# Rotary products read from PSUM by VectorE, sums by GpSimd, q/k/v parts stored by half sequences

## The chip, the cores and the metric

The kernel runs on one core of a Trainium2 chip, in one launch. The metric is the device time of that launch in microseconds (us), the median of three runs. Engines are named as the profile names them: PE is TensorE, PEld its weight loads, DVE VectorE, ACT ScalarE, POOL GpSimd, SP the SyncE queue that issues DMAs.

## The reference, cut to what matters

The kernel computes one attention layer and one mixture-of-experts layer on x of shape (8, 1024, 256), in float32. Only the front of the attention layer is touched by the change:

```python
x = x + attn(layernorm(x))                 # then x + ffn(layernorm(x)), 8 experts, top-k tokens
q, kv = x @ Wq, x @ Wkv                    # 16 heads of 16 columns; kv is both keys and values
q, kv = rotary(q), rotary(kv)              # per head: t * cos + rotate_half(t) * sin
# rotate_half(t) = concat(-t[8:16], t[0:8]) within a head
att = softmax(q @ kv.T * 16 ** -0.5); out = att @ kv; out @ Wout + bout
```

## The kernel before, in words

The program has five stages that follow each other on every engine: **project** (the one that changes), attend, finish, choose and experts. All orders are written out by hand, engine by engine, and semaphores join them.

`project` handles the 8 sequences as 64 tiles of 128 tokens, two sequences (16 tiles) to a pass, 4 passes. For a tile the steps are: statistics and normalisation on DVE (L231 to L244), two PE transposes into `p_ps_xT` (L373), a copy to SBUF by ACT (L338), four matmul passes (PE, L381) into a PSUM bank of `p_ps_q` that holds q and kv side by side (512 columns), a copy of that bank to `p_qkv` in SBUF (ACT, L345), the rotary, four PE transposes into `p_ps_rT` (L391), and the cutting of the result into a high and a low part: ACT copies the high part, rounded to float32r (L354), DVE subtracts it for the low part (L272). ACT also copies the values (L355). The rotary is shared out: DVE multiplies `p_qkv` by cos (L254), POOL multiplies the swapped halves by sin in two instructions (L307), and the sum is made by DVE for the first 128 columns (L264) and by POOL for the other 384 (L317).

The order on each engine is a software pipeline: in the period of tile j an engine does step A for tile j minus the lag of A, step B for tile j minus the lag of B, and so on (`Flow`, L73; the lags stand in L109). So each engine walks through its list once for every tile, and a wait in any step holds back the steps behind it on that engine.

The parts of a sequence lie in `p_parts`, which has room for two sequences. When all 8 tiles of a sequence are cut, SP stores them to the DRAM tensor `qkv_parts` with 8 DMAs of 512 KB (L178; 128 rows of 4 KB each; the DRAM side has 8 heads as its first dimension, 16 rows and 1024 elements) and then the values with one DMA of 1 MB (L182). ACT may write the first tile of a sequence only when the parts and values of the sequence two before have landed (L351, L352). SP is one queue in program order: it also loads x in blocks of four tiles (L167), and it issues `load_first` (L209), which loads the first three pairs of heads for the attend stage (L528, L534, and the rows of ones, L553). In the last pass `load_first` stands before the stores of that pass.

`attend` works on 64 pairs of heads. PE starts with the score maxima of pair 0 (L709, needs the loads of pair 0 and the end of the project stage on PE and DVE), DVE reduces them (L761), the maxima are turned into rows and put into `a_q` by a DMA that ACT issues for pair 0 (L543), and only then do the scores of pair 0 start (L672). For pair 1 the same DMA is issued by SP, which first waits for all stores of the project stage (`stored`, L213).

## Time and profile before

| | us |
|---|---|
| three runs, median (lowest to highest) | 2242.66 (2234.14 to 2255.21) |
| the profiled execution | 2249.14 |
| its span | 2247.3 |
| PE, DVE, ACT, POOL busy | 2015.3, 1947.7, 1503.4, 649.2 |
| last cut of the project stage (DVE, L272) | begins at 242.59 |
| first scores of the attend stage (PE, L672) | begin at 276.38 |

The busy figures are over the whole span; the project stage is its first ninth, which is why they say little of it. The page also cuts the span into 40 slices of 56 us: the first four and a half are the project stage. For a single stage one reads the views of that stretch: groups of instructions by line, busy time by windows, and the timeline of one engine.

### The profile page before, as it was taken

The page shows a single profiled execution, that of the slowest core. Times are in us where ns is not written, and L with a number is a line of the kernel's source. Part 1 is how long each engine was busy: PE and PEld are TensorE (multiplying, and loading weights), DVE is VectorE, ACT ScalarE, POOL GpSimd, SP SyncE. Part 2 cuts the span into 40 slices and gives each one's busy share as a digit, 9 for nine tenths or more (in the row PEclk, how much of TensorE's full clock was granted, in tenths as well). Part 3 has the DMA queues.
Part 4 walks back from the last instruction along what each step waited for, and adds up shares of the span by engine and source line. Part 5 has one row for each costly group of instructions (what it writes and reads, how often), then busy time and mean ns, then how long its engine had stood idle before and what let it go on. Part 6 is the DMA issues. An engine that isn't in the chain of part 4 may idle for free. (4 is left out here: it accounts for less than half of the span.)

```text
span 2247.3 us, 53242 instructions
## 1 busy us (share of the span) xinstructions
PE 2015.3 (90%) x16684; PEld 1046.1 (47%) x16684; DVE 1947.7 (87%) x3221; ACT 1503.4 (67%) x2842; POOL 649.2 (29%) x864
## 2 busy tenths in 40 slices
PE   6777699999999999999999999999898129999998
PEld 3333233333333333333333333333476118999997
DVE  7887879999999999999999999999299668888863
ACT  3444268888888888888888888888545004554443
POOL 7788201110110111011101110111277014555653
PEclk9999679999999999999999999999999559999999
DMA  2666632444344444433443444343486023433432
GB/s 89 219 224 204 182 92 69 83 82 77 71 83 83 74 74 81 85 73 75 82 85 70 78 81 80 72 80 71 145 273 202 23 85 74 105 87 90 98 68 29
DMA packets 152687, 224.69 MB, mean 100 GB/s; under 512 B 34871, under 2 KB 105114, under 8 KB 152602
## 3 DMA queue, kind: packets, MB, share of 16 engines
q1 hardware_dynamic: 131958, 197.96, 36.7%
q0 software_dynamic: 12288, 17.05, 4.5%
q10 hardware_dynamic: 8356, 8.67, 1.1%
q8 instruction: 39, 0.64, 0.1%
q14 instruction: 46, 0.38, 0.1%
HBM read 129.45 MB, written 93.06 MB: 99 GB/s over the span
## 5 line engine op out<-in xcount | busy, mean ns | idle before, releaser
L761 DVE TENSOR_REDUCE a_mx<-a_sm 128x2 f32<-128x1024 f32 x1024 | 1235.5, 1223 | 69.6 <-PE a_sm L709 54.0
L836 ACT ACTIVATE a_prob<-a_st 128x512 f32<-128x512 f32 x2048 | 1113.2, 597 | 180.5 <-PE a_st L672 150.0
L709 PE MATMUL a_sm<-a_k,a_q 48*128 48x512 f32 x2048 | 759.1, 460 | 9.3 <-DVE a_mx L761 7.6
L672 PE MATMUL a_st<-a_q,a_k 50*128 50x512 f32 x2048 | 761.3, 452 | 5.8 <-DMA a_q<-a_mrow 5.8
L696 PE MATMUL a_pv<-a_prob,a_v 128*32 128x256 f32 x8192 | 660.7, 394 | 22.9 <-ACT a_oraw L843 22.3
L672 PEld LDWEIGHTS a_st<-a_q,a_k 50*128 50x128 f32 x2048 | 313.0, 187 | 415.0 <-ACT a_prob L836 395.5
L696 PEld LDWEIGHTS a_pv<-a_prob,a_v 128*32 128x32 f32 x8192 | 162.2, 108 | 404.7 <-issue 198.1
L811 POOL TENSOR_TENSOR a_v<-a_v_raw,a_zero 128x256 f32<-128x256 f32 x64 | 39.6, 620 | 1052.5 <-DMA a_v_raw<-values 1002.9
L709 PEld LDWEIGHTS a_sm<-a_k,a_q 48*128 48x128 f32 x2048 | 306.2, 189 | 21.2 <-DVE a_mx L761 19.2
L1751 ACT ACTIVATE e_hT<-e_ps_h,e_b1b 128x512 f32<-128x512 f32 x128 | 88.3, 690 | 207.5 <-PE e_ps_h L1788 203.8
L1788 PE MATMUL e_ps_o<-e_w_high,e_hT_high 128*128 128x256 f32 x512 | 145.9, 285 | 0.0
L1788 PE MATMUL e_ps_o<-e_w_high,e_hT_low 128*128 128x256 f32 x512 | 144.8, 283 | 0.0
L1788 PE MATMUL e_ps_o<-e_w_low,e_hT_high 128*128 128x256 f32 x512 | 144.8, 283 | 0.0
L381 PE MATMUL p_ps_q<-p_w,p_xnT 128*128 128x512 f32 x256 | 126.2, 617 | 0.0
L1704 POOL TENSOR_TENSOR e_ahead<-e_row_no 128x1 f32<-128x1 f32 x72 | 48.6, 675 | 254.9 <-DVE e_idx L1597 167.1
L1641 DVE TENSOR_TENSOR e_hT_low<-e_hT,e_hT_high 128x512 fp32r<-128x512 f32 x128 | 86.6, 691 | 40.5 <-ACT e_hT_high L1757 40.5
L1727 POOL DMA_INDIRECT out_dram<-e_ob,e_idx x64 | 112.3, 1754 | 13.9 <-issue 8.7
L1788 PE MATMUL e_ps_h<-e_yT_high,e_w_high 128*128 128x512 f32 x256 | 101.8, 398 | 0.0
L1788 PE MATMUL e_ps_h<-e_yT_low,e_w_high 128*128 128x512 f32 x256 | 101.1, 395 | 0.0
L1788 PE MATMUL e_ps_h<-e_yT_high,e_w_low 128*128 128x512 f32 x256 | 100.7, 393 | 0.0
L345 ACT COPY p_qkv<-p_ps_q 128x512 f32<-128x512 f32 x64 | 37.5, 586 | 94.3 <-PE p_ps_q L381 50.2
L307 POOL TENSOR_TENSOR p_tsin<-p_qkv,p_sin 128x256 f32<-128x256 f32 x128 | 98.1, 786 | 3.7 <-ACT p_qkv L345 3.7
(146 smaller groups left out, 2362.5 us busy)
## 6 DMA issues: line engine op xcount, KB each, us to landing
qkv_parts<-p_parts SPq DMA_DIRECT2D x64, 512.0 KB
a_q<-qkv_parts SPq DMA_DIRECT2D x128, 128.0 KB, 3.5
a_k<-qkv_parts SPq DMA_DIRECT2D x128, 128.0 KB, 4.3
attended<-a_oraw SPq DMA_DIRECT2D x64, 256.0 KB, 3.9
e_w<-in_fc_dram SPq DMA_DIRECT2D x16, 1024.0 KB, 5.2
token_table<-f_tab ACTq DMA_DIRECT2D x8, 1056.0 KB, 4.9
p_x<-in_x_dram SPq DMA_DIRECT2D x16, 512.0 KB, 8.5
values<-p_values SPq DMA_DIRECT2D x8, 1024.0 KB, 20.2
```

The lines of the kernel that those rows point to most:

```text
L307: nc.gpsimd.tensor_tensor(ts[:, :, h * HALF:(h + 1) * HALF], src[:, :, (1 - h) * HALF:(2 - h) * HALF], sinb[:, i:i + 1, h * HALF:(h + 1) * ...
L381: mm = nc.tensor.matmul(ps_q[:, k % 2], xnT[:, k % 2, c], w[:, c], start=(c == 0), stop=(c == DC - 1))
L672: nc.tensor.matmul(st[:, slot % RING], kb[rows, q.buf, jt * P:(jt + 1) * P], qb[rows, q.buf, ic * CHUNK:(ic + 1) * CHUNK], start=True, sto ...
L696: mm = nc.tensor.matmul(pv[row:row + 2 * DH, cols], vb[:, q.buf, jt, h, :], prob[:, jt % 2, h, start:start + QUARTER], start=(jt == 0 and ...
L709: mm = nc.tensor.matmul(sm[:, slot, h], qb[rows, q.buf, qt * P:(qt + 1) * P], kb[rows, q.buf, kc * CHUNK:(kc + 1) * CHUNK], start=True, st ...
L761: nc.vector.tensor_reduce(mx[:, qt, kc, :], sm[:, slot], AX.X, ALU.max, negate=True).then_inc(max_done, 1)
L836: nc.scalar.activation(prob[:, jt % 2, h, ic * CHUNK:(ic + 1) * CHUNK], st[:, slot % RING], ACT.Exp, scale=DH ** -0.5).then_inc(drained, 1)
L1641: nc.vector.tensor_tensor(group_of(hT_low, g), hT[:, g % 4], group_of(hT_high, g), ALU.subtract).then_inc(hT_low_done, 1)
L1704: nc.gpsimd.tensor_tensor(ahead[:], row_no[:], row_no[:], ALU.add).then_inc(ahead_done, 1)
L1727: nc.gpsimd.indirect_dma_start(out=out_rows, out_offset=bass.IndirectOffsetOnAxis(ap=idx[:, k, i:i + 1], axis=0), in_=ob[:, i], in_offset= ...
L1751: nc.scalar.activation(hT[:, g % 4], ps_h[:, g % 3], ACT.Gelu_apprx_tanh, bias=b1b[:, k, g % FC:g % FC + 1]).then_inc(gelu_done, 1)
L1788: return nc.tensor.matmul(to, weights, moving, start=first, stop=last)
```

## The change: what it does

- **Weights.** The columns of `w_qkv` are put in half-major order on the host: first the lower halves (8 columns) of all 32 heads of q and kv, then the upper halves. The sine table changes sign between its halves.
- **Rotary.** ACT no longer copies `p_ps_q` to SBUF; `p_qkv` is gone. DVE reads the PSUM bank twice, once times cos and once times sin, 512 columns each. POOL makes only the sums, in two instructions of 256 columns, which also put the columns back into head order. DVE has no part of the sum any more.
- **Banks and lags.** `p_ps_q` gets four banks instead of two. ACT's copy of the turned tokens, the transposes back, the high part and the low part each come one or two periods later; PE's order within a period stays.
- **Stores.** Parts are stored by half sequences: 8 DMAs of 256 KB (rows of 2 KB) after every 4 tiles, 128 DMAs in all instead of 64. Values are stored as before, once a sequence. SP's loop is written out, with x loads between the half stores, and `load_first` comes after the two half stores of the first sequence of the last pass and its values, where it came before them.

```diff
-    NORM, PROJ, TURN, SUM, BACK, CUT = 6, 7, 8, 9, 10, 11
-    FIRST = P
+    NORM, TURN, TURNED, PROJ, ROTATE, SUM, BACK, HIGH, CUT = 6, 6, 7, 8, 9, 10, 11, 12, 13
+    QBANKS = 4
...
-    ps_q = mem.ps("p_ps_q", [P, 2, 4 * P])
+    ps_q = mem.ps("p_ps_q", [P, QBANKS, 2 * D])
...
-        def store(it, s):
-
-            done = it * STEP + (s + 1) * TILES
+        def store(it, h):
+
+            done = it * STEP + (h + 1) * GROUP
+            s, cols = h // 2, slice(h % 2 * GROUP * P, (h % 2 + 1) * GROUP * P)
             sp.wait_ge(high_done, done)
             sp.wait_ge(low_done, done)
             for c in range(4):
                 kind, chunk = c // 2, c % 2
                 for part in range(CUTS):
-                    sp.dma_start(
-                        parts_dram[bass.ds((it * SEQS + s) * H + chunk * 8, 8), kind, part],
-                        parts[:, s, c, part].bitcast(F32)).then_inc(parts_out[s], 16)
...
+                    first = (it * SEQS + s) * H + chunk * 8
+                    sp.dma_start(parts_dram[first:first + 8, kind, part, :, cols],
+                                 parts[:, s, c, part, cols].bitcast(F32)).then_inc(parts_out[h], 16)
+            if h % 2 == 1:
+                sp.wait_ge(values_done, done)
+                sp.dma_start(v_dram[it * SEQS + s].rearrange("r p n -> p r n"),
+                             values[:, s].rearrange("p r i h e -> p r (i h e)")).then_inc(v_out[s], 16)
...
+        for it in range(PASSES):
+            for h in range(GROUPS):
+                if it > 0:
+                    store(it - 1, h)
+                if h < 2 and it > 0:
+                    load(it, h + 2)
+                elif h >= 2 and it + 1 < PASSES:
+                    load(it + 1, h - 2)
+        for h in range(GROUPS):
+            if h == 2:
+
+                for first in range(2):
+                    sp.wait_ge(parts_out[first], 16 * 4 * CUTS)
+                sp.wait_ge(v_out[0], 16)
+                load_first(sp)
+            store(PASSES - 1, h)
...
-            nc.vector.tensor_tensor(t_cos[:, k % 2].rearrange("p (h d) -> p h d", d=DH),
-                                    qkv[:, k % 2].rearrange("p (h d) -> p h d", d=DH),
-                                    cosb[:, i:i + 1, :].to_broadcast([P, 2 * H, DH]),
+                dve.wait_ge(rot_done, 2 * (n - 1))
+            nc.vector.tensor_tensor(t_cos[:, k % 2].rearrange("p (x d) -> p x d", d=HALF),
+                                    ps_q[:, k % QBANKS].rearrange("p (x d) -> p x d", d=HALF),
+                                    cosb[:, i:i + 1, 0:HALF].to_broadcast([P, 4 * H, HALF]),
                                     ALU.mult).then_inc(cos_done, 1)
...
+            nc.vector.tensor_tensor(t_sin[:, k % 2].rearrange("p (o x d) -> p o x d", o=2, d=HALF),
+                                    ps_q[:, k % QBANKS].rearrange("p (o x d) -> p o x d", o=2, d=HALF),
+                                    sinb[:, i].rearrange("p (o d) -> p o d", o=2).unsqueeze(2)
+                                    .to_broadcast([P, 2, 2 * H, HALF]), ALU.mult).then_inc(sin_done, 1)
...
+            for h in range(2):
+                to = rot[:, k % 2].rearrange("p (x h d) -> p x h d", h=2, d=HALF)[:, :, h]
+                own, other = (buf[:, k % 2, of * D:(of + 1) * D].rearrange("p (x d) -> p x d", d=HALF)
+                              for buf, of in ((t_cos, h), (t_sin, 1 - h)))
+                nc.gpsimd.tensor_tensor(to, own, other, ALU.add).then_inc(rot_done, 1)
...
-        def projected(it, k, n):
-            act.wait_ge(q_done, n + 1)
-            if past(n, 2):
-
-                act.wait_ge(rot_done, n - 1)
-            nc.scalar.copy(qkv[:, k % 2], ps_q[:, k % 2]).then_inc(qkv_done, 1)
-
         def high_part(it, k, n):
             s, i = k // TILES, k % TILES
+            if k % GROUP == 0 and past(it):
+
+                act.wait_ge(parts_out[k // GROUP], 16 * 4 * CUTS * it)
             if i == 0 and past(it):
-
-                act.wait_ge(parts_out[s], 16 * 4 * CUTS * it)
                 act.wait_ge(v_out[s], 16 * it)
```

How the written order moves is seen at two places. First SP, before, from the stores of the last sequence of pass 2 (the next to last pass) on; the eight rows that load a pair of heads are shown as their first four, and the rows of the other pairs are left out.

```order
L178 DMA qkv_parts<-p_parts 8x16x1024 [waits p_low_done,p_high_done]
L178 DMA qkv_parts<-p_parts 8x16x1024 x7
L182 DMA values<-p_values 128x8x256 [waits p_values_done]
L547 DMA a_ident<-in_ident_dram 128x128 [waits p_v_out0,p_parts_out0]
L528 DMA a_q<-qkv_parts 32x1024
L528 DMA a_q<-qkv_parts 16x1024
L528 DMA a_k<-qkv_parts 16x1024
L528 DMA a_k<-qkv_parts 32x1024
...
L553 DMA a_k<-a_ones 2x24x128
L178 DMA qkv_parts<-p_parts 8x16x1024 [waits p_low_done,p_high_done]
```

The same stretch of SP in the changed kernel, from the values of that same sequence on:

```order
L181 DMA values<-p_values 128x8x256 [waits p_values_done]
L177 DMA qkv_parts<-p_parts 8x16x512 [waits p_low_done,p_high_done]
L177 DMA qkv_parts<-p_parts 8x16x512 x7
L177 DMA qkv_parts<-p_parts 8x16x512 [waits p_low_done,p_high_done]
L177 DMA qkv_parts<-p_parts 8x16x512 x7
L181 DMA values<-p_values 128x8x256 [waits p_values_done]
L524 DMA a_ident<-in_ident_dram 128x128 [waits p_v_out0,p_parts_out1,p_parts_out0]
L505 DMA a_q<-qkv_parts 32x1024
L505 DMA a_q<-qkv_parts 16x1024
L505 DMA a_k<-qkv_parts 16x1024
L505 DMA a_k<-qkv_parts 32x1024
```

Between the values of pass 2 and the first load of the attend stage there now stand 16 stores of parts (two halves) and one of values, which stood behind it before.

Second DVE, one period in the middle of a pass, before:

```order
L231 BN_STATS p_stats<-p_x 128x6
L244 TENSOR_SCALAR p_xn<-p_x,p_mv,p_rstd 128x256
L254 TENSOR_TENSOR p_tcos<-p_qkv,p_cos 128x512
L272 TENSOR_TENSOR p_parts<-p_ps_rT,p_parts 128x4x128
L264 TENSOR_TENSOR p_rot<-p_tcos,p_tsin 128x128
```

and in the changed kernel:

```order
L228 BN_STATS p_stats<-p_x 128x6
L241 TENSOR_SCALAR p_xn<-p_x,p_mv,p_rstd 128x256
L251 TENSOR_TENSOR p_tcos<-p_ps_q,p_cos 128x512
L255 TENSOR_TENSOR p_tsin<-p_ps_q,p_sin 128x512
L265 TENSOR_TENSOR p_parts<-p_ps_rT,p_parts 128x4x128
```

The short sum has gone, and a second product of full width has come in its place, behind the first.

## Rows read from the trace of the kernel before

**Rows 1.** The page's part 2, 40 slices of the whole span, two of its rows.

```profile
PEclk9999679999999999999999999999999559999999
DMA  2666632444344444433443444343486023433432
```

**Rows 2.** Groups of instructions from 0 to 243.4 us: busy us, mean ns, idle before.

```profile
L381 PE MATMUL p_ps_q<-p_w,p_xnT 128*128 128x512 f32 x256 | 126.2, 617 | 0.0
L307 POOL TENSOR_TENSOR p_tsin<-p_qkv,p_sin 128x256 f32<-128x256 f32 x128 | 98.1, 786 | 3.7 <-ACT p_qkv L345 3.7
L317 POOL TENSOR_TENSOR p_rot<-p_tcos,p_tsin 128x384 f32<-128x384 f32 x64 | 72.9, 1138 | 36.2 <-ACT p_values L355 33.6 <-POOL p_tsin L307 0.5
L254 DVE TENSOR_TENSOR p_tcos<-p_qkv,p_cos 128x512 f32<-128x512 f32 x64 | 63.9, 998 | 21.2 <-ACT p_qkv L345 21.2
...
L272 DVE TENSOR_TENSOR p_parts<-p_ps_rT,p_parts 128x512 fp32r<-128x512 f32 x64 | 43.5, 680 | 16.6 <-ACT p_parts L354 16.6
...
L244 DVE TENSOR_SCALAR p_xn<-p_x,p_mv,p_rstd 128x256 f32<-128x256 f32 x64 | 37.6, 588 | 0.6 <-POOL p_rstd L295 0.6
...
L231 DVE BATCH_NORM_STATS2 p_stats<-p_x 128x6 f32<-128x256 f32 x64 | 26.2, 415 | 1.6 <-DMA p_sin<-in_rot_sin_dram 1.6
```

**Rows 3.** Waits of ACT up to 313 us: us in total, times, longest.

```profile
ACT p_qkv L345 <- POOL p_rot L317: 44.0, 30, 2.2
...
ACT p_parts L354 <- DMA values<-p_values: 17.7, 5, 5.6
```

**Rows 4.** Windows: length; busy time of PE, PEld, DVE, ACT, POOL; PEclk, DMA share, GB/s.

```profile
314.72:315.40 0.68, 0.68 (x8) 0.30 (x12) 0.29 (x1) 0.33 (x2) 0.04 (x1) 1.00 0.97 367
57.00:64.00 7.00, 5.10 (x20) 2.71 (x20) 6.40 (x13) 3.66 (x9) 6.61 (x8) 1.00 0.51 209
...
66.00:72.00 6.00, 5.05 (x21) 2.72 (x20) 4.82 (x10) 2.81 (x7) 5.79 (x8) 1.00 0.92 229
```

**Rows 5.** Timeline of SP's queue: start us, us taken, instruction, how many.

```profile
50.23 12.55 SPq L178 DMA_DIRECT2D qkv_parts<-p_parts  x8
62.83 1.56 SPq L182 DMA_DIRECT2D values<-p_values  x1
...
204.21 2.31 SPq L182 DMA_DIRECT2D values<-p_values  x1
206.62 11.90 SPq L547 DMA_DIRECT2D a_ident<-in_ident_dram  x1
...
224.82 0.88 SPq L528 DMA_DIRECT2D a_k<-qkv_parts  x2
...
301.40 1.41 SPq L543 DMA_DIRECT2D a_q<-a_mrow  x2
```

**Rows 6.** The tile p_values: landing of the eight stores of values.

```profile
DMA to landing us min/median/max: 18.8/20.2/23.0
```

**Rows 7.** Timeline of DVE: the cuts of tiles 0, 7 and 63.

```profile
26.20 0.68 DVE L272 TENSOR_TENSOR p_parts<-p_ps_rT,p_parts 128x512 fp32r<-128x512 f32 x1
...
49.47 0.68 DVE L272 TENSOR_TENSOR p_parts<-p_ps_rT,p_parts 128x512 fp32r<-128x512 f32 x1
...
242.59 0.69 DVE L272 TENSOR_TENSOR p_parts<-p_ps_rT,p_parts 128x512 fp32r<-128x512 f32 x1 [2.08 <-ACT p_parts L354]
```

**Rows 8.** The page's part 6: issues, KB each, median us to landing.

```profile
a_k<-qkv_parts SPq DMA_DIRECT2D x128, 128.0 KB, 4.3
```

**Rows 9.** Timeline of PE and ACT where the attend stage starts.

```profile
243.54 1.22 PE L709 MATMUL a_sm<-a_k,a_q 48*128 48x512 f32 x4 [1.60 <-DVE p_parts L272]
...
264.30 3.96 ACTq L543 DMA_DIRECT2D a_q<-a_mrow  x2
...
276.38 0.76 PE L672 MATMUL a_st<-a_q,a_k 50*128 50x512 f32 x1 [5.84 <-DMA a_q<-a_mrow]
```

**Rows 10.** Windows over the first two pairs of the attend stage, columns as in rows 4.

```profile
276.40:313.00 36.60, 36.60 (x203) 12.55 (x203) 21.37 (x19) 19.34 (x37) 0.45 (x2) 0.52 0.39 124
313.00:338.00 25.00, 24.29 (x237) 9.15 (x233) 23.77 (x22) 22.01 (x42) 1.08 (x3) 1.00 0.36 69
```

More of the change, by code:

```diff
@@ L137, in project @@
     x_in = [a.sem(f"p_x_in{g}") for g in range(GROUPS)]
-    parts_out = [a.sem(f"p_parts_out{s}") for s in range(SEQS)]
+    parts_out = [a.sem(f"p_parts_out{h}") for h in range(GROUPS)]
     v_out = [a.sem(f"p_v_out{s}") for s in range(SEQS)]
@@ L201, in sync, with stored @@
             load(0, g)
-        body(0)
-        with sp.Fori(1, PASSES - 1) as it:
-            body(it)
-        store(PASSES - 2, 1)
-        sp.wait_ge(parts_out[0], 16 * 4 * CUTS)
-        sp.wait_ge(v_out[0], 16)
-        load_first(sp)
+        for it in range(PASSES):
+            for h in range(GROUPS):
+                if it > 0:
+                    store(it - 1, h)
[10 more added lines that the diff above has]
+            store(PASSES - 1, h)
+    def stored(sp):
+        for h in range(GROUPS):
+            sp.wait_ge(parts_out[h], 16 * 4 * CUTS * PASSES)
         for s in range(SEQS):
-            store(PASSES - 1, s)
-    def stored(sp):
-        for s in range(SEQS):
-            sp.wait_ge(parts_out[s], 16 * 4 * CUTS * PASSES)
             sp.wait_ge(v_out[s], 16 * PASSES)
@@ L275, in body @@
         def body(it, j):
-            for stage, lag in ((statistics, 0), (normalise, NORM), (cos_product, TURN), (low_part, CUT),
-                               (first_sum, SUM)):
+            for stage, lag in ((statistics, 0), (normalise, NORM), (rotate, ROTATE), (low_part, CUT)):
                 tile = flow.at(it, j, lag)
@@ L295, in inverse_root, with add @@
             nc.gpsimd.tensor_tensor(rstd[:, cols], veps[:, cols], mhalf[:], ALU.pow).then_inc(rstd_done, 1)
-        def turn(it, k, n):
-            i = k % TILES
-            src = qkv[:, k % 2].rearrange("p (h d) -> p h d", d=DH)
-            ts = t_sin[:, k % 2].rearrange("p (h d) -> p h d", d=DH)
-            pool.wait_ge(qkv_done, n + 1)
-            if past(n, 2):
-                pool.wait_ge(rot_done, n - 1)
-                pool.wait_ge(rot_first_done, n - 1)
-            for h in range(2):
-                nc.gpsimd.tensor_tensor(
-                    ts[:, :, h * HALF:(h + 1) * HALF], src[:, :, (1 - h) * HALF:(2 - h) * HALF],
-                    sinb[:, i:i + 1, h * HALF:(h + 1) * HALF].to_broadcast([P, 2 * H, HALF]),
-                    ALU.mult).then_inc(sin_done, 1)
+        def add(it, k, n):
             pool.wait_ge(cos_done, n + 1)
-            pool.wait_ge(sin_done, n * 2 + 2)
+            pool.wait_ge(sin_done, n + 1)
             if past(n, 2):
@@ L316, in turn @@
                 pool.wait_ge(values_done, n - 1)
-            nc.gpsimd.tensor_tensor(rot[:, k % 2, FIRST:], t_cos[:, k % 2, FIRST:], t_sin[:, k % 2, FIRST:], ALU.add
-                                    ).then_inc(rot_done, 1)
+            for h in range(2):
[3 more added lines that the diff above has]
+                nc.gpsimd.tensor_tensor(to, own, other, ALU.add).then_inc(rot_done, 1)
         def body(it, j):
@@ L323, in body @@
                 inverse_root(*tile)
-            tile = flow.at(it, j, TURN)
+            tile = flow.at(it, j, SUM)
             if tile:
-                turn(*tile)
-        pool.wait_ge(consts_in, 64)
+                add(*tile)
         pool.wait_ge(halves_set, 2)
-        flow.run(pool, body, TURN)
+        flow.run(pool, body, SUM)
     def scalar(act):
@@ L359, in body @@
         def body(it, j):
-            for stage, lag in ((turned_tokens, NORM), (projected, PROJ), (high_part, BACK)):
+            for stage, lag in ((turned_tokens, TURNED), (high_part, HIGH)):
                 tile = flow.at(it, j, lag)
@@ L394, in body @@
         def body(it, j):
-            for stage, lag in ((turn_tokens, NORM), (products, PROJ), (turn_back, BACK)):
+            for stage, lag in ((turn_tokens, TURN), (products, PROJ), (turn_back, BACK)):
                 tile = flow.at(it, j, lag)
```

53 lines of the change are left out of this document (16 added, 37 removed).

## The prediction

> **What bounds the kernel now.** The page's slices come first [rows 1]. The change touches only the project stage, the first four and a half slices; after it every stage runs the same instructions. What counts is the moment at which the attend stage starts its scores, 276.38 us [rows 9]. If that moves by d, the end moves by d.
>
> Inside the stage I read the groups [rows 2]. Per tile POOL spends 2 x 0.786 + 1.138 = 2.71 us, and ACT waits 44.0 us for it [rows 3], so POOL's chain looks like the bound, and it is what the change relieves. The cuts of tiles 0 and 7 start at 26.20 and 49.47 us [rows 7]: 3.32 us a tile, 26.6 us a sequence of eight, when nothing else holds.
>
> But the second line of the waits names another bound: ACT stands 17.7 us in 5 waits for the values store of the sequence two before [rows 3]. The values are issued at 62.83 and, five sequences later, at 204.21 us [rows 5]: 28.3 us a sequence, more than the 26.6 of the engines. Each lands 20.2 us after its issue [rows 6]. And the windows show why: from 57 to 64 us, with stores of parts alone in flight, the 16 DMA engines are busy 0.51 and move 209 GB/s [rows 4]. That is eight engines that never rest while eight have nothing. A sequence's 4.19 MB of parts take 4.19/209 = 20.1 us there, and 1.05 MB of values and 1.05 MB of x fill the rest. **The stores bound the stage, with POOL just beneath them.**
>
> **The change, part by part.**
>
> *Rotary.* ACT loses a copy, POOL falls to two sums of 256 columns, the size of L307: 2 x 0.786 = 1.57 us a tile. DVE loses its short sum and gets a second product. No row shows a product from PSUM. L272 reads one operand from PSUM and one from SBUF, 512 columns, 0.680 us; L254 reads both from SBUF, 0.998 us [rows 2]. I take the nearer, L272, and keep 0.998 for a rival. DVE's sum is then 0.415 + 0.588 + 3 x 0.680 = 3.04 us, some 3.1 with the small ones; no engine has more. A gain of 0.2 us a tile, 13 us over 64 tiles, if nothing else bound. PE's four passes and transposes are those of before. The lags grow by two periods, so the first cut comes at about 29 us (the filling periods are short), and tile 3's ends at 29 + 3 x 3.1 + 0.7 = 39 us (37 to 41).
>
> *First store.* It goes at 39 us, where SP issued it at 50.23 [rows 5]: 11.2 us sooner. This is the real gain, since the queue hardly rests from then on.
>
> *Rows of 2 KB.* 314.72 to 315.40 us holds a store of 2 KB rows on all engines: 367 GB/s at 0.97, or 23.6 GB/s an engine; the 4 KB rows have 209/(16 x 0.51) = 25.6 [rows 4]. On eight engines a sequence's parts would take 22.2 us instead of 20.1, so the price is 0 (bytes alone) to 2.1 us a sequence; I take 1.5, nearer the row, which is short. The Trainium skill, page "DMA: Bandwidth & Descriptors", section "Rules for kernel authors", asks for at least 1 MiB a DMA, and its section "Anatomy of one DMA — SWDGE (gpsimd) path" puts about 2 us on each one; 64 more DMAs would by that add 128 us if nothing covered them. The row from 57 to 64 us speaks against a serial charge: share and rate stay whole across DMAs that follow each other.
>
> *Queue up to pass 2.* Values of sequence 5 landed at 204.21 + 20.2 = 224.4 us. Now: 224.4 - 11.2 + 6 x 1.5 + 1.4 for one more x load behind the first store (0.52 MB at 367 GB/s) = 223.6. The first tile of the last sequence is let go there; before, its last cut ended 242.59 + 0.69 - 224.4 = 18.9 us later, so the engines finish near 243, as they did. **The faster rotary is hidden behind the stores.**
>
> *load_first.* Here the change costs. Before, the loads of pair 0 stood right behind the values of sequence 5. The last of them was issued at 224.82 to 225.7 us, and such a load lands in 4.3 [rows 5, 8]: 230, which is 5.6 us behind those values and 13 us before PE wanted them at 243.54 [rows 9]. Now sixteen stores and the values of sequence 6 stand between. They need 28.3 + 1.5 less two x loads of 1.4 = 27.0 us, so they land at 250.6, and pair 0's loads 5.6 us later, at 256.2. PE starts the maxima 256.2 - 243.5 = 12.7 us later than before. What covered the loads were the stores behind them, and these have changed places with them.
>
> *After it.* ACT's DMA of the maxima went at 264.30 and its data released PE at 276.38, 12.1 us for 16 KB among rows of 4 KB [rows 9]. Beside rows of 2 KB it may be as slow or half as long: 0 to 6 us saved, I take 3. Pair 1 needs all stores landed; SP was through with that by 301.40 [rows 5], 77.0 us after sequence 5. The same count from 223.6 and two sequences of 1.5 gives 303.6, and pair 1's scores start only at 313.0 + 9.7: no cost.
>
> **Sum.** +12.7 - 3 = +9.7 us. On the profiled execution 2249.14 + 9.7 = 2258.8; that execution is 6.5 us above the median of the three runs, so against the median 2242.66 + 9.7 = **2252 us**. Its own bounds: first store at 37, nothing for short rows and 6 saved give 224.4 - 13.2 + 1.4 = 212.6, then 212.6 + 25.5 + 5.6 = 243.7, so 0.2 - 6 = -6; first store at 41, 2.1 a sequence and nothing saved give 229.2, then 229.2 + 27.6 + 5.6 = 262.4, so +19. That is 2237 to 2262.
>
> **Rivals.**
> - *The queue gets tighter* (chance 0.15). ACT's wait comes in halves and SP fills the queue every four tiles; if pauses in it vanish, the loads land by 240 and the engines' end rules, some 5 us earlier than now: 2242.66 - 5 - 3 = 2235.
> - *The engines rule alone* (0.06). If the stores kept up, the last cut would end at 29 + 63 x 3.1 + 0.7 = 225 us, 18 us sooner, and with PE's and POOL's fastest beat of some 2.9 us at 212, 31 us sooner: 2225 to 2212. It needs stores on more than eight engines. The written order speaks against it: the DRAM side stays eight heads wide, 8x16x1024 and now 8x16x512. The Trainium skill, the same DMA page, section "Why a DMA increments its semaphore by 16 and not by 1", says that the first dimensions of both sides decide how many engines a DMA gets; the share of 0.51 agrees.
> - *DVE becomes the bound, the slow side* (0.10). If a product costs what L254 costs, 0.998 us, with groups of 8 columns or POOL in its way, a tile takes 0.1 + 0.415 + 0.588 + 2 x 0.998 + 0.680 = 3.8 us, and the last cut ends at 29 + 63 x 3.8 + 0.7 = 269 us. Attend starts 25.6 us later: 2268; at 1.2 us a product, 4.2 a tile, 2293. It decides from (256.2 - 29.7)/63 = 3.6 us a tile, 0.9 us a product. For it: L254 mostly costs more than L272. Against it: L272 itself, with POOL busy beside it.
> - *SP's issuing becomes the bound* (0.07). Eight stores took 12.55 us to issue and values 1.56 [rows 5]. Sixteen are 25.1, with values and two x loads 29.8, just what the queue needs. If SP waits between, say 2 us a sequence, 7 sequences add 14: 2266.
> - *Each DMA pays its latency in the queue* (0.02). A load of 128 KB lands in 4.3 us [rows 8], of which 0.36 us is data at 367 GB/s. If each of the 64 added DMAs paid the other 3.9 one after the other, the end would come 250 us later, 2492. The unbroken share of 0.51 speaks against it.
> - My forecast has the other 0.60.
>
> **Range and chances.** Pair 0 ran at half clock (0.52, the 1.2 GHz level) in 36.6 us, pair 1 at full clock in 25.0 [rows 10]: a clock that rises sooner or later moves the end by up to 11.6 us either way, and three runs of the same kernel lay between 2234 and 2255. Joined to 2237 to 2262 and the nearer rivals this gives 2230 to 2270. About 1%, 22 us, is what can be told from no change. Faster by that needs the engines alone: 0.07. Slower takes most of DVE's case, half of SP's, the full DMA charge and the top end of the forecast with a bad clock: 0.15. Within it: 0.78.
>
> **What would show it.** Right: the first store issued near 39 us; values a sequence apart by 28 to 30 us; a DMA share near 0.51 with parts alone in flight, at 189 to 209 GB/s; ACT waiting longer for values or parts; the last cut near 243; PE idle before its first maxima, released by a load of a_q or a_k near 256; the products near 0.68 us; POOL's sums near 0.79. Wrong: no idle time before the maxima, or a DMA share well above 0.51 with parts alone, or a cadence under 27 us (then it gains); products above 0.9 us (then it loses more).

## The result and the profile after

The changed kernel took 2238.2 us (median of 19 runs, 2226.72 to 2245.58) beside 2245.61 us for the kernel before on the same chip (19 runs, 2234.14 to 2255.21): a ratio of 0.9962, 95% interval 0.9946 to 0.9978. The medians are 7.4 us apart, the ratio says 8.5: some 8 us faster. A second measurement (after_again, below) gave 0.9966 (0.9947 to 0.9985). That is within 1% and inside the range of the prediction, but the sign is wrong: +9.7 us was forecast.

The profiled execution has a span of 2242.4 us against 2247.3. First the moment that counts, on the timeline of PE; it answers to [rows 9].

```profile
241.75 1.22 PE L686 MATMUL a_sm<-a_k,a_q 48*128 48x512 f32 x4 [14.36 <-DMA a_k<-qkv_parts]
...
270.04 0.76 PE L649 MATMUL a_st<-a_q,a_k 50*128 50x512 f32 x1 [1.28 <-DMA a_q<-a_mrow]
```

The brackets say how long the engine was idle and what ended it. Before, PE waited 1.60 us for the last cut; now it waits 14.36 us for a load of `a_k`, as forecast, but from an earlier point: the maxima start 1.8 us sooner than at 243.54 instead of 12.7 later, and the scores 6.3 us sooner than at 276.38. ACT's issue of the maxima stands between the two (start us, us taken):

```profile
262.52 1.94 ACTq L520 DMA_DIRECT2D a_q<-a_mrow  x2
```

It released PE 7.5 us later, where it had taken 12.1.

SP's timeline tells how the queue got there; it answers to [rows 5].

```profile
37.62 8.97 SPq L177 DMA_DIRECT2D qkv_parts<-p_parts  x8
...
56.33 1.17 SPq L181 DMA_DIRECT2D values<-p_values  x1
...
198.37 1.24 SPq L181 DMA_DIRECT2D values<-p_values  x1
...
226.75 1.28 SPq L181 DMA_DIRECT2D values<-p_values  x1
228.14 3.28 SPq L524 DMA_DIRECT2D a_ident<-in_ident_dram  x1
```

The first store goes 12.6 us sooner than at 50.23. Five sequences after 56.33, at 198.37, the values are issued again, 28.4 us a sequence, practically the 28.3 of before. The tile `p_values`, taken from 195 to 215 us, says when these landed:

```profile
DMA to landing us min/median/max: 11.6/11.6/11.6
```

So they landed at 210.0, where before it was 224.4 and 223.6 was forecast. They let go the first tile of the last sequence on ACT, which had waited 0.21 us for them. Before, ACT reached that tile at 224.66 and did not wait for the values at all (the second line). DVE's last cut ends 18.8 us after the landing, at the same distance as before:

```profile
210.07 0.59 ACT L329 CAST p_parts<-p_ps_rT 128x512 fp32r<-128x512 f32 x1 [0.21 <-DMA values<-p_values]
```

```profile
224.66 0.59 ACT L354 CAST p_parts<-p_ps_rT 128x512 fp32r<-128x512 f32 x1
```

```profile
228.05 0.69 DVE L265 TENSOR_TENSOR p_parts<-p_ps_rT,p_parts 128x512 fp32r<-128x512 f32 x1 [2.13 <-ACT p_parts L329]
```

The groups of instructions, 0 to 230 us (busy us, mean ns, idle before), answer to [rows 2].

```profile
L300 POOL TENSOR_TENSOR p_rot<-p_tcos,p_tsin 128x256 f32<-128x256 f32 x128 | 91.4, 735 | 97.8 <-ACT p_values L330 74.1 <-DVE p_tsin L255 22.8 <-DVE p_tcos L251 0.9
...
L251 DVE TENSOR_TENSOR p_tcos<-p_ps_q,p_cos 128x512 f32<-128x512 f32 x64 | 43.9, 686 | 18.4 <-PE p_ps_q L358 10.7 <-POOL p_rot L300 7.7
L255 DVE TENSOR_TENSOR p_tsin<-p_ps_q,p_sin 128x512 f32<-128x512 f32 x64 | 43.5, 679 | 0.0
L265 DVE TENSOR_TENSOR p_parts<-p_ps_rT,p_parts 128x512 fp32r<-128x512 f32 x64 | 43.4, 680 | 3.6 <-ACT p_parts L329 3.6
...
L228 DVE BATCH_NORM_STATS2 p_stats<-p_x 128x6 f32<-128x256 f32 x64 | 26.2, 416 | 24.4 <-DMA p_x<-in_x_dram 22.5 <-DMA p_sin<-in_rot_sin_dram 2.0
```

The products cost what was forecast, 0.68 us; the sums cost 0.735 us, a little less than the 0.786 put in. New is the last line: DVE stands 22.5 us for x, which it did not before.

The page's slices, the answer to [rows 1], and the window with stores of parts alone, the answer to [rows 4]:

```profile
PEclk9899579999999999999999999999998559999999
DMA  4666623344334434443444344343485023433432
```

```profile
188.00:199.00 11.00, 10.66 (x37) 5.77 (x36) 8.12 (x21) 3.96 (x10) 5.50 (x8) 0.84 0.53 204
```

The DMA digits are sixes again, a share near 0.6, but begin sooner. 2 KB rows move 204 GB/s on eight engines, 2% less than the 209 of before, not the 10% less that the price of 2.1 us stood for.

### The profile page after: what moved, and what is told of

The parts are those of the page before. It is cut to its first block and busy times, and to the rows that moved or that the text cites. A ratio compares the mean times of both kernels' runs of the same rounds, so it can differ in the third digit from the quotient of the medians.

```text
span 2242.4 us, 52901 instructions
## 1 busy us (share of the span) xinstructions
PE 2021.2 (90%) x16684; PEld 1046.7 (47%) x16684; DVE 1931.4 (86%) x3221; ACT 1476.0 (66%) x2778; POOL 574.7 (26%) x800
## 5 line engine op out<-in xcount | busy, mean ns | idle before, releaser
L673 PE MATMUL a_pv<-a_prob,a_v 128*32 128x256 f32 x8192 | 661.2, 395 | 23.0 <-ACT a_oraw L820 22.4
L300 POOL TENSOR_TENSOR p_rot<-p_tcos,p_tsin 128x256 f32<-128x256 f32 x128 | 91.4, 735 | 97.8 <-ACT p_values L330 74.1
L319 ACT COPY p_xnT<-p_ps_xT 128x256 f32<-128x256 f32 x64 | 23.8, 373 | 123.3 <-PE p_ps_q L358 111.9
## 6 DMA issues: line engine op xcount, KB each, us to landing
values<-p_values SPq DMA_DIRECT2D x8, 1024.0 KB, 12.3
```

Source lines behind the costliest of these rows:

```text
L300: nc.gpsimd.tensor_tensor(to, own, other, ALU.add).then_inc(rot_done, 1)
L673: mm = nc.tensor.matmul(pv[row:row + 2 * DH, cols], vb[:, q.buf, jt, h, :], prob[:, jt % 2, h, start:start + QUARTER], start=(jt == 0 and ...
```

## The experiments

Each ran in 5 rounds beside the kernel before; "ratio" is to that kernel. Its median lay between 2237.0 and 2245.0 us in these groups, so totals of different rows compare only by their ratios; where an expectation names a total, read it so. The last three columns (us) are from one profiled execution each. Where an edit repeats one already shown, only the addition is given.

| run | median us | ratio (95% interval) | last cut begins | first maxima | first scores |
|---|---|---|---|---|---|
| early_load | 2221.08 | 0.9925 (0.9897 to 0.9953) | 231.14 | 232.08 | 263.61 |
| late_load | 2246.94 | 1.0042 (1.0027 to 1.0058) | 243.79 | 261.35 | 290.28 |
| halves_only | 2233.94 | 0.9979 (0.9960 to 0.9998) | 232.28 | 241.70 | 270.18 |
| rotary_only | 2268.78 | 1.0135 (1.0112 to 1.0159) | 277.10 | 278.04 | 309.78 |
| rotary_cut_first | 2236.66 | 0.9979 (0.9966 to 0.9992) | 234.15 | 235.10 | 268.96 |
| halves_early | 2228.15 | 0.9941 (0.9919 to 0.9963) | 229.07 | 230.01 | 261.37 |
| after_again | 2235.37 | 0.9966 (0.9947 to 0.9985) | 232.64 | 243.00 | 271.76 |
| split_rows | 2222.60 | 0.9930 (0.9909 to 0.9951) | 230.69 | 231.63 | 264.00 |
| split_far | 2231.92 | 0.9934 (0.9912 to 0.9956) | 229.85 | 230.79 | 263.52 |
| split_new | 2224.33 | 0.9898 (0.9872 to 0.9924) | 226.57 | 227.51 | 258.25 |
| early_cut_first | 2221.06 | 0.9902 (0.9870 to 0.9935) | 219.88 | 220.83 | 252.78 |
| wide_old_rotary | 2218.22 | 0.9910 (0.9888 to 0.9933) | 226.16 | 227.11 | 253.90 |
| wide | 2198.88 | 0.9798 (0.9776 to 0.9820) | 201.25 | 202.19 | 229.03 |
| wide_early_cut_first | 2189.95 | 0.9784 (0.9762 to 0.9805) | 197.53 | 198.47 | 225.26 |

Before, the first scores began at 276.38. In all these rows and in the changed kernel the ratio, turned into us, follows the shift of the first scores to within 5 us. In single executions the rest is looser: from the first scores to the end of the span they took 1955.6 (early_load) to 1972.9 us (after_again), 1970.9 before and 1972.4 in the changed kernel. So a difference in total of a few us between two rows can't be put down to the project stage alone.

### The place of the attend stage's loads

**early_load**, the changed kernel with

```diff
-            if h == 2:
+            if h == 0:
                 for first in range(2):
                     sp.wait_ge(parts_out[first], 16 * 4 * CUTS)
                 sp.wait_ge(v_out[0], 16)
                 load_first(sp)
```

> The changed kernel with one thing moved: the loads of the attend stage stand ahead of all stores of the last pass, as they did before the change. Theory 'the place in the queue': in the changed kernel PE idled 14.4 us before its first maxima (241.75 us) for loads that stood behind the stores of sequence 6, while the last cut was over at 228.7. So the maxima begin at 229 to 231, ACT's DMA of the maxima goes 11 us sooner, and it waits 8 to 12 us for its data; the attend stage's first scores begin at 257 to 262 (270.04 in the changed kernel), the total is 8 to 12 us below the changed kernel, 2226 to 2230. Rival 'given back': the loads in front delay the stores of the last pass and with them the last cut (to 235 or later) or pair 1 (which waits for all stores), and the total falls by less than 4 us.

The wait for the loads is gone and the run gains 0.4% more, about 8 us, the lower end of what was expected. Part of the 11 us is given back: the maxima start 9.7 us sooner, since the last cut is 3 us later, and the DMA of the maxima takes 10.8 us instead of 7.5. The first scores, at 263.61, come just behind the expected 257 to 262. PE's timeline:

```profile
232.08 1.22 PE L686 MATMUL a_sm<-a_k,a_q 48*128 48x512 f32 x4 [1.60 <-DVE p_parts L265]
...
263.61 0.76 PE L649 MATMUL a_st<-a_q,a_k 50*128 50x512 f32 x1 [4.54 <-DMA a_q<-a_mrow]
```

**late_load**, the kernel before with

```diff
-        load_first(sp)
         for s in range(SEQS):
+            if s == 1:
+                load_first(sp)
             store(PASSES - 1, s)
```

> The kernel before with one thing moved: the loads of the attend stage stand behind the stores of sequence 6, as in the change. Theory 'the place in the queue' (the price of +12.7 us in the prediction): values of sequence 5 land at 224.4 as before, the maxima begin 31 us later (the distance seen in the changed kernel), at 254 to 257, released by a load of a_q or a_k, and the total rises by 8 to 13 us, to 2252 to 2257. Rival 'it costs nothing': the loads land before the last cut is over (243.3) and the total is that of the kernel before within 2 us.

It costs 0.42%, 9.4 us, inside the 8 to 13 that were expected. PE shows the wait:

```profile
261.35 1.22 PE L710 MATMUL a_sm<-a_k,a_q 48*128 48x512 f32 x4 [18.22 <-DMA a_k<-qkv_parts]
...
290.28 0.76 PE L673 MATMUL a_st<-a_q,a_k 50*128 50x512 f32 x1 [1.93 <-DMA a_q<-a_mrow]
```

The maxima start 17.8 us later than before, and at 261.35 they miss the expected 254 to 257. But here too the DMA of the maxima is quick, 8.2 us, with rows of 4 KB beside it. On eight engines, from ACT's issue to the first scores, it took 10.0 to 13.1 us in the nine executions with these loads early and 7.5 to 8.2 in the four with the loads late. So most of its saving comes from the order and not, as I had argued, from the short rows; among the early ones rows of 2 KB have 10.0 to 12.0 us and rows of 4 KB 11.0 to 13.1, about 1 us apart on average. With the stores on sixteen engines (wide, below) it took 6.0 to 6.1 us, loads early or late.

### The two halves of the change apart

**halves_only**: the kernel before with SP's program, `parts_out` and ACT's wait for it as in the change.

> The old rotary (ACT's copy to SBUF, sin products on POOL, sum shared) with SP's whole program of the change: half-sequence stores, loads one sequence later. Theory 'the queue alone': first store issued at 37 us (tile 3 is cut at 26.2 + 3 x 3.32 + 0.7), values a sequence apart by 28 to 29 us, maxima within 3 us of 241.75, the total that of the changed kernel within 3 us (2235 to 2241). Rival 'the engines have a share': with 3.32 us a tile instead of 2.7 the stores run dry between sequences, the cadence is over 29 us, the last cut is later than 235, and the total is at least 4 us above the changed kernel.

**rotary_only**: the changed kernel with SP's program, `parts_out` and ACT's wait for it as before.

> The new rotary and lags with SP's whole program of before: stores of whole sequences in rows of 4 KB, loads ahead of the last pass. Theory 'the queue alone': tile 7 is cut at 28.8 + 7 x 2.7 + 0.7 = 48.4, so the first store goes at 48.5 us instead of 50.23, everything behind it 1.8 us sooner: last cut at 239 to 241, first scores near 274.5, total 0 to 3 us below the kernel before (2242 to 2245). ACT's DMA of the maxima still waits about 12 us, if the rows of 4 KB beside it are what slows it; 7 to 8 us if it was not the rows. Rival 'the engines have a share': the total falls by 6 us or more, as the change as a whole did.

The stores alone bring the first scores to 270.18, where the whole change has 270.04 and 271.76, and their ratio of 0.9979 can't be told from its 0.9962 and 0.9966 (the intervals overlap). With the old rotary their last cut comes at 232.28. That is nearly the engines' own pace, (232.28 - 25.48)/63 = 3.28 us a tile from a first cut at 25.48, where the kernel before has 3.32 within a sequence; with the new rotary the engines are faster but wait for x and values, and end no sooner than 228 to 233. The new rotary alone loses 1.35%, about 30 us: neither theory had that. Its values go 35.8 us apart. DVE's timeline shows why, in the period in which sequence 2's last tile is cut:

```profile
118.00 0.43 DVE L229 BATCH_NORM_STATS2 p_stats<-p_x 128x6 f32<-128x256 f32 x1 [11.44 <-DMA p_x<-in_x_dram]
118.35 0.86 DVE L242 TENSOR_SCALAR p_xn<-p_x,p_mv,p_rstd 128x256 f32<-128x256 f32 x1
119.13 0.68 DVE L252 TENSOR_TENSOR p_tcos<-p_ps_q,p_cos 128x512 f32<-128x512 f32 x1
119.73 0.67 DVE L256 TENSOR_TENSOR p_tsin<-p_ps_q,p_sin 128x512 f32<-128x512 f32 x1
120.33 0.67 DVE L266 TENSOR_TENSOR p_parts<-p_ps_rT,p_parts 128x512 fp32r<-128x512 f32 x1
```

The cut has a lag of 13 now. For the last tile of a sequence that is the period whose first instruction is the statistics of a new block of x (7 + 13 = 20, a multiple of 4; with the old lag it was 18). That block lands behind the stores and values of the sequence before, so the cut, and with it the next stores, wait for them; SP issues the next stores at 121.28. This was a theory made after the run, so it got one of its own.

**rotary_cut_first**, rotary_only with one line of DVE's order changed:

```diff
-            for stage, lag in ((statistics, 0), (normalise, NORM), (rotate, ROTATE), (low_part, CUT)):
+            for stage, lag in ((low_part, CUT), (statistics, 0), (normalise, NORM), (rotate, ROTATE)):
```

> The new rotary with SP's program of before and, as the only other edit, DVE's cut put ahead of the statistics within a period. Theory 'the cut behind the x load': with the lag of 13 the cut of a sequence's last tile stands in the same period as the statistics of the next block of x, and that block lands only behind the stores and values of the sequence before, so cuts and stores take turns (35.6 us a sequence in the run with the new rotary alone). With the cut in front the cadence of the values falls to 27 to 30 us and the total to that of the kernel before within 5 us, 2235 to 2245. Rival 'the lags or the two PSUM products are slow in themselves, or rows of 4 KB behind longer lags': the cadence stays above 33 us and the total at 2262 or more.

All the loss goes: 2236.66 us, 28.7 us a sequence. The new lag, with the cut behind the statistics, was the cause. DVE waits 61.7 us for x in rotary_only and 22.5 in the changed kernel. I put the difference down to the x loads that the change has between its half stores; no run separates them from the half stores themselves. Nor is the changed kernel free of the trap: early_cut_first, below, is early_load with this one line changed, and its last cut comes 11.3 us sooner (219.88 against 231.14).

### Which theory of the queue: sixteen engines

**wide**: within a chunk of 8 heads the weight columns are ordered by dimension and then head, so that row r*8+h of the parts is dimension r of head h. The tables are broadcast over the 8 heads, the values are copied in two pieces, and

```diff
-                    sp.dma_start(parts_dram[first:first + 8, kind, part, :, cols],
+                    sp.dma_start(parts_dram[first:first + 8, kind, part, :, cols].rearrange("h r n -> r h n"),
```

> The changed kernel with the columns inside a chunk ordered dimension-major (16 dimensions, then 8 heads), so that each store of parts has 16 rows of heads as its first dimension on the DRAM side (16x8x512 instead of 8x16x512); bytes, row length of 2 KB and count of DMAs are the same; the values are copied by ACT in two instructions, POOL subtracts in one of its two instructions. Theory 'eight engines bound the stores': with stores alone in flight the DMA share rises from about 0.52 to over 0.85 and the rate to 330 GB/s or more; a sequence's 6.3 MB take 17 to 19 us; the engines then set the pace, 2.7 to 2.9 us a tile, the last cut comes at 205 to 215, and PE's first maxima with it, since the loads land before; the total falls by 25 to 35 us below the changed kernel, to 2203 to 2213. Rival 'the HBM side or the queue's issuing is the bound': the rate stays under 250 GB/s and the total within 5 us of the changed kernel. SP's issuing (16 stores x 1.1 us and three others, 21 to 29 us a sequence when it isn't blocked) may stop the gain halfway: last cut 220 to 235.

It is 2% faster than before, some 37 us below the changed kernel beside it; last cut and total came even sooner than expected. The values go 22.4 us apart, 2.8 us a tile:

```profile
55.31 0.68 SPq L181 DMA_DIRECT2D values<-p_values  x1
...
189.94 0.65 SPq L181 DMA_DIRECT2D values<-p_values  x1
```

That is six sequences from 55.31 to 189.94. The page's slices of this run, the stage in the first three and a half:

```profile
PEclk9997699999999999999999999999997559999999
DMA  4989243443444343343343344343484033333432
```

The DMA share has gone to 8 and 9 tenths, and between 208 and 220 us, when the stores of the last sequence and the loads fill the queue, the windows show share and rate:

```profile
208.00:220.00 12.00, 8.44 (x22) 2.88 (x20) 12.00 (x11) 0.00 (x0) 0.62 (x1) 0.50 1.03 318
```

The 330 GB/s that were expected come only from 212 us on, when the loads have been issued: 369 from 212 to 220. So the eight engines were the limit. The rivals "HBM side" and "issuing" fall: the bytes and the row length are the same, and here SP issues eight stores in 5.9 us, where the changed kernel took 9.0, waiting for the queue. The Trainium skill, page "DMA: Bandwidth & Descriptors", section "Why a DMA increments its semaphore by 16 and not by 1", gives a DMA as many engines as the largest number up to 16 that divides the slowest dimension of both sides; share and rate of this run agree.

**wide_old_rotary**: halves_only with the same row order and 16x8x512 stores, on the old rotary.

> The old rotary (ACT's copy, sin products on POOL) with the half-sequence stores on 16 engines (16x8x512): what the new rotary is worth once the stores don't bound. Theory 'the rotary was hidden behind the stores': the engines set the pace at 3.2 to 3.4 us a tile, the values come 26 to 27 us apart (22.4 with the new rotary), the last cut at 230 to 238 (201.25 with the new rotary), the total at 2222 to 2232, so 25 to 33 us above the new rotary with the same stores. Rival 'the new rotary is no faster': last cut within 5 us of 201 and the total under 2205.

The cadence is 26.2 us; last cut and total are each 4 us earlier than the expected ranges. It is 0.9910 where the new rotary has 0.9798: the faster rotary is worth 25 us once the stores stand aside, and nothing that can be measured while they don't. **halves_early** is halves_only with the loads placed as in early_load:

> The old rotary with the half-sequence stores and the loads of the attend stage ahead of the last pass: what the new rotary is worth when nothing holds PE behind the last cut. Theory 'the rotary counts only after the last gate': the last cut is about 4 us later than in the changed kernel with early loads (232.28 against 228.05 without them), so the maxima begin at 235 to 237 and the total is 3 to 5 us above that kernel (2221), 2224 to 2227. Rival 'the new rotary counts nowhere': the same total within 2 us.

0.9941 against 0.9925 for the new rotary; the intervals overlap, so on eight engines the totals leave this unresolved. The first theory fails in its mechanism: the last cut comes at 229.07, 2 us before that of the new rotary (231.14) and not 4 after it.

### The price of rows of 2 KB

**split_rows**, the kernel before with its waits raised to twice the count and

```diff
-                    sp.dma_start(
-                        parts_dram[bass.ds((it * SEQS + s) * H + chunk * 8, 8), kind, part],
-                        parts[:, s, c, part].bitcast(F32)).then_inc(parts_out[s], 16)
+                    for cols in (slice(0, N // 2), slice(N // 2, N)):
+                        sp.dma_start(
+                            parts_dram[bass.ds((it * SEQS + s) * H + chunk * 8, 8), kind, part, :, cols],
+                            parts[:, s, c, part, cols].bitcast(F32)).then_inc(parts_out[s], 16)
```

> The kernel before with one edit: each store of 512 KB in rows of 4 KB becomes two of 256 KB in rows of 2 KB, issued one behind the other at the same place. It measures the term of the prediction that was taken as +1.5 us a sequence (0 to 2.1). Theory 'short rows are nearly free': windows of the changed kernel show 204 GB/s against 209, so 0.5 us a sequence at most; cadence of the values 28.3 to 28.9, last cut at 243 to 247, total 0 to 4 us above the kernel before. Rival 'the prediction's price': cadence 29.8 us, the values of sequence 5 are issued 7 to 8 us later than at 204.21, the last cut comes at 251 or later, and the total rises by 8 to 11 us. The values should land about 12 us behind their issue, not 20, if the queue holds a number of packets and not of bytes.

Both theories are wrong: the split makes the kernel 0.7% faster, 16 us by the ratio. The values go 26.7 us apart, which is the engines' own 26.6:

```profile
69.89 1.21 SPq L183 DMA_DIRECT2D values<-p_values  x1
...
203.44 1.41 SPq L183 DMA_DIRECT2D values<-p_values  x1
```

These are five sequences. Windows of the kernel before, then of this one, in the stretch of a sequence where values and x move beside stores; then this one with stores alone:

```profile
94.00:100.00 6.00, 5.03 (x22) 2.73 (x21) 5.17 (x16) 3.07 (x8) 5.54 (x8) 1.00 0.91 250
```

```profile
98.00:106.00 8.00, 5.51 (x23) 3.03 (x24) 7.96 (x19) 3.99 (x9) 7.02 (x9) 1.00 0.98 312
84.00:96.00 12.00, 9.48 (x40) 5.17 (x39) 10.41 (x24) 6.24 (x15) 11.00 (x14) 1.00 0.53 203
```

With stores alone the short rows are a little slower (203 against 209 GB/s), as forecast. But beside values and x the queue now moves 312 GB/s instead of 250. The values also land 10.4 us after their issue instead of 20.2. Most of that is only that SP issues them later: those of the first sequence go 7.1 us later (69.89 instead of 62.83) and land 2.8 us sooner. Over 84 to 196 us the rates are, before and split:

```profile
84.00:196.00 112.00, 84.25 (x320) 44.57 (x320) 93.66 (x199) 53.25 (x125) 92.45 (x112) 0.97 0.66 219
```

```profile
84.00:196.00 112.00, 85.65 (x336) 45.14 (x334) 99.30 (x209) 56.68 (x134) 98.36 (x119) 1.00 0.66 231
```

The last two numbers are share and rate: at the same share 5% more bytes. The two windows are no chance picks. Taking windows of 2 us from 60 to 200 us and averaging those with a share of at least 0.85 (mixed) and those under 0.56 (about the eight engines), in one execution each:

| run | mixed, GB/s | under 0.56, GB/s |
|---|---|---|
| before | 258 | 191 |
| split_rows | 307 | 200 |
| changed kernel | 305 | 187 |

Whether the mixed stretch gains by the shorter rows or by the smaller DMAs these runs don't tell. The Trainium skill, same page, section "Rules for kernel authors", asks for DMAs of at least 1 MiB; here halving 512 KB made the kernel faster, and the measurement decides.

**split_far**: the same 16 stores, with `for cols` as the outermost loop.

> The 16 stores of 2 KB rows of a sequence as in the run with split rows (2222.6 us, 231 GB/s between 84 and 196 us), but in another order: first the 8 with the left halves of all rows, then the 8 with the right halves, which lie half a sequence's stores apart, as in the changed kernel. Nothing else. Theory 'the two halves of a row belong together': with the halves apart the rate falls to that of the changed kernel (216 to 221 GB/s), the cadence rises from 26.7 to 28 or more, the last cut comes at 236 to 242 and the total at 2230 or more. Rival 'the interleaved x loads or SP's order of the half stores make the difference': rate, cadence and total stay as with split rows, 2220 to 2226, and the last cut at 230 to 232.

231 GB/s, 26.6 us a sequence, last cut at 229.85 and the same ratio: the rival holds, and the order of the halves among themselves is free. (The total, 2231.92, lies above the rival's 2220 to 2226; the kernel before beside it was 5.5 us slower too, 2242.57 against 2237.04.) That left the changed kernel (28.4 us a sequence) to be explained:

```profile
84.00:196.00 112.00, 88.83 (x320) 46.52 (x318) 86.73 (x197) 39.79 (x96) 55.04 (x79) 0.91 0.65 221
```

Two runs were made for it: **split_new**, rotary_cut_first with the stores of split_rows, and **early_cut_first**, early_load with the cut in front.

> The new rotary, DVE's cut ahead of the statistics, SP's program of before with each store split into two of 2 KB rows. Against the same with rows of 4 KB (2237, 28.7 us a sequence, last cut 234.15). Theory 'the queue serves split rows faster, whatever the engines do': rate 228 to 235 GB/s between 84 and 196 us, cadence 26.7 to 27.5, first store at 44.9, so the last cut comes at 224 to 228 and the total is 7 to 12 us below the run with 4 KB rows, 2225 to 2230. Rival 'the new rotary itself slows the transfers': rate 215 to 221, cadence over 28, last cut over 231, total 2233 or more.

> The changed kernel with early loads of the attend stage and DVE's cut ahead of the statistics; it differs from split_new only in SP's order (half sequences with x loads between them, against whole sequences). Theory 'the half-sequence order costs rate': 214 to 222 GB/s and 28 us or more a sequence, but the first store goes at 34 us instead of 45; the last cut comes at 226 to 231 and the total at 2217 to 2224. If the order costs nothing (rival), rate and cadence are those of split_new (26.7 to 27.5 us), and 11 us of head start remain: last cut at 213 to 218, total 2205 to 2210.

The same window of split_new and of early_cut_first:

```profile
84.00:196.00 112.00, 90.47 (x331) 48.02 (x330) 87.22 (x204) 41.15 (x98) 57.18 (x82) 0.92 0.65 226
```

```profile
84.00:196.00 112.00, 88.57 (x321) 46.65 (x320) 85.82 (x199) 40.41 (x96) 54.61 (x79) 0.92 0.66 221
```

split_new fits its first theory nearly throughout: 27.4 us a sequence, last cut 226.57, and 0.8% faster than the same with rows of 4 KB (0.9898 against 0.9979); its rate of 226 is below the 228 expected, its total 0.7 us below the range, and the first store went 1.3 us later. early_cut_first has the rate (221) and the total (2221.06) of its first theory, 28.0 us a sequence at that theory's edge, and a last cut, 219.88, between the two. So of the 231 GB/s the half-sequence order with its x loads in between costs some 5, in one execution of each, and the new rotary may cost as much again. By the table above the changed kernel has the whole gain in the mixed stretches, 305 GB/s, and loses it in the others, 187 instead of 200. That is as far as it is shown; why those stretches are slower stays open. One candidate that no run separates is PE's clock: over 84 to 196 us it is 1.00 in split_rows, 0.92 in the last two runs and 0.91 in the changed kernel. In the totals split_new and early_cut_first can't be told apart.

**after_again** is the changed kernel, unedited:

> The changed kernel itself, unedited, so that the others of this call and the old rotary with the new stores (2234) have it beside them on the same chip: a ratio to the kernel before of 0.995 to 0.998, first maxima at 241 to 243, released by a load of a_q or a_k.

It came out so, at 0.9966 and 243.00.

**wide_early_cut_first** is wide with early loads and the cut in front:

> The new rotary with stores on 16 engines, the loads of the attend stage ahead of the last pass, and DVE's cut ahead of the statistics: a candidate for the fastest version. Theory: with 16 engines PE's first maxima were already released by the last cut and not by a load, so moving the loads gives nothing more; the cut in front makes the first cut 3.5 us earlier (25.35 against 28.85 with the new rotary and stores of before), so the last cut comes at 197 to 202 and the total is 0 to 5 us below 2199. Rival: the loads still held something (the copies of the maxima, pair 1), and the total falls by more than 6 us.

2189.95 us, 0.9784 (0.9762 to 0.9805), the lowest time of all, with its last cut at 197.53, as expected. The total is 9 us below 2199, which looks like the rival, but by the ratios it is 3 us below wide (0.9798), and that is less than the intervals resolve. It beats both kernels by far more than the change itself: about 47 us below before.

## Why the prediction was wrong, step by step

- *Stores bound, on eight engines*: right, shown by wide. What it missed is that the queue's 28.3 us a sequence were no fixed cost: split_rows brought them to 26.7 with the same engines and bytes.
- *Rotary*: right in the price of the product (0.68 us), 7% high in that of the sum (0.735 us for 0.786), and right that it is hidden: halves_only has the same first scores. Not seen was the lag of 13, which with SP's program of before costs 30 us (rotary_only). DVE's sum of 3.04 us was too high as a pace, because it adds durations of instructions that overlap: in DVE's timeline of rotary_only above, products of 0.67 us follow each other every 0.60 us, and wide keeps 2.8 us a tile, with DVE busy 126.7 of the 130 us from 60 to 190. That didn't matter while the stores bound.
- *First store at 39*: 37.62, 12.6 us sooner instead of 11.2; right.
- *Rows of 2 KB, +1.5 us a sequence*: **the step that failed.** From first store to the landing of sequence 5's values the forecast was 174.2 of before + 9.0 for rows + 1.4 for an x load = 184.6 us; it took 172.4. Those 12.2 us are nearly all of the 14.5 by which the maxima came sooner than 256.2 (241.75). The cadence did not rise by 1.5 us a sequence but by 0.1. The price was taken from 0.68 us of another stage, with stores alone; the range 0 to 2.1 left no room for a gain, although nothing in the trace excluded one. Measured alone, the split was worth -0.7% in the kernel before, by the stretch where values and x move beside stores. In the changed kernel most of that gain is lost again, as the last two runs indicate, and the cadence stays at 28.4. The 2 us a DMA that the prediction quotes from the Trainium skill stand in the section on DMAs that GpSimd issues, and the stores here are SP's; 64 more of them added nothing that can be seen.
- *Engines finish near 243*: wrong as its consequence. The 18.9 us from the landing to the end of the last cut were right to 0.1 (18.8), in part by luck: ACT stood 0.21 us at that gate now and not at all before, so at this tile the engines arrive together with the values, and the waits that held the stage lie in the sequences ahead of it.
- *load_first, 32.6 us from the landing to the maxima*: 31.8, released by a load; right. By itself it costs 9.4 us (late_load) and taking it back gains 8 (early_load).
- *The DMA of the maxima, -3 us*: -4.6, inside its 0 to 6, mostly wrong in reason: late_load has 8.2 us with rows of 4 KB. It is luck that the size came out.
- *Pair 1, no cost*: SP's issue for pair 1 went at 295.06 instead of 301.40, by the same 6.3 us as the scores; right.
- *Sum*: +12.7 - 3 should have been -1.8 - 4.6 = -6.4 at the first scores; the medians say -7.4, the ratio -8.5.
- *Rivals*: "the queue gets tighter" named this outcome's sign and nearly its number (loads by 240, 2235; they landed at 241.7), with a chance of 0.15. Its mechanism did not show: the values go 28.4 us a sequence apart, no closer than before, so what came true is the earlier first store without the price of the short rows. "The engines rule alone" put the last cut at 212 to 225 us; with sixteen engines it came at 201.94 (wide), below that, for the overlap on DVE named above. DVE as the bound, SP's issuing and a latency for each DMA all fell: 64 more DMAs, in split_rows and in the change alike, made nothing slower.

## What to carry to other kernels

Ask first how many engines a store really gets, and what its leading dimension is: reordering rows so that 16 stands in front took 37 us off the changed kernel, where the whole change had brought 8. Price a queue over a full cycle of its mixed traffic, not by a window with one kind of transfer alone, and let the bound of an unknown row length reach to a gain too. Read an engine's pace from the starts of its instructions, not from the sum of their durations. When lags grow, look in which period each step that others wait for now falls, and which load's wait stands ahead of it.

## What was not expected of the hardware

- Eight engines with 4 KB rows beside other traffic on all sixteen moved 229 GB/s at a share of 0.92 [rows 4] and 250 at 0.91 (window above), 250 to 260 on average over the four executions with such rows; with rows of 2 KB it was 312 at 0.98, 292 to 312 on average over nine.
- After such a burst the rate can fall below that of stores alone. A window of the changed kernel:

```profile
96.00:102.00 6.00, 1.26 (x6) 0.50 (x4) 1.34 (x3) 1.26 (x3) 2.39 (x4) 0.78 0.51 162
```

  That is half the share with 162 GB/s, where stores alone have 203 to 209, and PE is busy 1.26 of 6 us. Why it falls is not shown. PE's granted clock is 0.78 there and 0.50 from 100 to 106 us, its lower level, after PE had stood idle; before, the clock was 0.97 over the whole of 84 to 196 us, now it is 0.91. So here a stall for data also cost clock.
- The same 1 MB of values took 20.2 us from issue to landing before, 12.3 in the changed kernel, 10.4 in split_rows and, with the stores on 16 engines, 6.8 (medians): time to landing depends on what is in the queue, not on the transfer alone.
